# A block-local attention kernel: the last three slots of the last batch and all that follows get a written-out order on all five engines, over more PSUM banks

## The reference

```python
def attn(x, Wq, bq, Wk, bk, Wv, bv, Wo, bo):      # x: 8 x 1024 x 256, 16 heads of 16
    q, k, v = (x @ W.T + b, split into heads)
    scores = einsum('bqhd,bkhd->bhqk', q, k) * 0.25
    mask = (j <= i) & (j >= i - 128)
    scores = where(mask, scores, -10000.0)
    p = softmax(scores) + 1e-9
    return einsum('bhqk,bkhd->bqhd', p, v) @ Wo.T + bo
x = x + attn(layernorm(x), ...)
x = x + einsum('bsi,oi->bso', layernorm(x), sign(weight))
```

## Time and profile before

| | us |
|---|---|
| median of 3 runs | 717.18 |
| the runs | 714.24, 717.18, 721.31 |
| the profiled execution's time | 716.17 |
| its span in the trace | 714.4 |
| PE busy | 668.4 (94%) |
| DVE / ACT / POOL busy | 493.9 / 485.6 / 458.0 |
| mean granted TensorE clock | 0.992 |

### The profile page before, as it was taken

The page is one execution under the profiler, slowest core; times in us unless marked ns, Lnnn a source line. Parts: engine busy times, 40 slices in busy tenths (PEclk is TensorE's granted clock), DMA queues, the critical chain, the costliest instruction groups (busy, mean ns, idle before and its releaser), DMA issues.

```text
span 714.4 us, 31680 instructions
## 1 busy us (share of the span) xinstructions
PE 668.4 (94%) x13152; PEld 595.7 (83%) x13152; DVE 493.9 (69%) x1043; ACT 485.6 (68%) x1061; POOL 458.0 (64%) x651
## 2 busy tenths in 40 slices
PE   7789999999999999999999999999999999998875
PEld 6667988888888888898898888889898889886764
DVE  5566766777777767787777777777677877765435
ACT  4357776777768667777767677677667777674651
POOL 8936565677656567766666677566567756664662
PEclk9989999999999999999999999999999999999999
DMA  5948776796677677677676786767577757866411
GB/s 150 129 78 134 108 121 122 126 137 117 125 115 135 118 117 128 133 129 118 124 131 127 117 130 118 123 121 129 115 127 137 129 105 122 138 114 83 75 39 45
DMA packets 94942, 83.76 MB, mean 117 GB/s; under 512 B 10416, under 2 KB 94800, under 8 KB 94800
## 3 DMA queue, kind: packets, MB, share of 16 engines
q1 hardware_dynamic: 93354, 80.38, 65.8%
q10 hardware_dynamic: 1446, 1.35, 0.6%
HBM read 18.22 MB, written 8.39 MB: 37 GB/s over the span
## 4 chain that ended last, share of the span: by engine, by line
PE 73%; DMA 10%; SPq 6%; issue 4%; DVE 4%; ACT 2%; POOL 1%; DVEq 0%; POOLq 0%; ACTq 0%
PE gc L966 17%; PE sc L1102 16%; PE pv L1118 12%; PE ga L966 10%; DMA q_stack<-nmax_t 8%; SPq L271 5%; PE mx L1057 5%; PE mx L1063 4%; PE ga L1131 3%; PE gc L981 2%; DVE nmax L754 2%; PE gb L1146 2%; PE gb L1166 2%; DMA q_stack<-q_hi 1%; DVE x L814 1%
## 5 line engine op out<-in xcount | busy, mean ns | idle before, releaser
L561 ACT ACTIVATE prob<-sc 128x512 f32<-128x512 f32 x448 | 259.5, 599 | 103.3 <-PE sc L1102 99.5
L754 DVE TENSOR_REDUCE nmax<-mx 128x6 f32<-128x960 f32 x189 | 197.1, 1043 | 68.0 <-PE mx L1063 64.8
L1102 PE MATMUL sc<-q_stack,k_stack 128*128 128x256 f32 (+1 forms) x1024 | 210.8, 304 | 8.6 <-DMA q_stack<-nmax_t 3.5
L1102 PEld LDWEIGHTS sc<-q_stack,k_stack 128*128 128x128 f32 x1024 | 150.0, 191 | 24.5 <-DMA q_stack<-nmax_t 8.3
L434 POOL TENSOR_SCALAR ve<-mv 128x1 f32<-128x1 f32 x64 | 14.2, 222 | 206.5 <-DVE mv L826 205.3
L419 POOL TENSOR_SCALAR_AFFINE_SELECT prob<-prob 128x1024 f32<-128x1024 f32 x128 | 140.0, 1093 | 1.7 <-ACT prob L563 1.7
L416 POOL TENSOR_SCALAR_AFFINE_SELECT prob<-prob 128x1024 f32<-128x1024 f32 x112 | 122.4, 1093 | 11.9 <-ACT prob L561 11.6
L1118 PE MATMUL pv<-prob,v_ones 128*32 128x128 f32 x3840 | 119.6, 274 | 2.9 <-issue 2.2
L1118 PEld LDWEIGHTS pv<-prob,v_ones 128*32 128x32 f32 x3840 | 101.5, 110 | 12.2 <-issue 2.9
L1063 PE MATMUL mx<-k_max,q_stack 16*32 16x160 bf16 x4032 | 71.1, 229 | 3.3 <-issue 3.3
L792 DVE TENSOR_TENSOR ct_lo<-gb,ct_hi 128x256 fp32r<-128x256 f32 x64 | 26.8, 419 | 46.1 <-ACT ct_hi L578 46.1
(11 more groups left out here) (169 smaller groups left out, 1410.5 us busy)
## 6 DMA issues: line engine op xcount, KB each, us to landing
q_stack<-q_hi SPq DMA_DIRECT2D x128, 128.0 KB, 3.9
k_stack<-k_hi SPq DMA_DIRECT2D x128, 128.0 KB, 4.6
xs<-x SPq DMA_DIRECT2D x32, 256.0 KB, 4.2
q_stack<-q_lo SPq DMA_DIRECT2D x64, 128.0 KB, 4.9
k_stack<-k_lo SPq DMA_DIRECT2D x64, 128.0 KB, 4.4
xr<-x SPq DMA_DIRECT2D x64, 128.0 KB, 2.1
out<-x SPq DMA_DIRECT2D x64, 128.0 KB, 2.4
k_max<-k SPq DMA_DIRECT2D x64, 64.0 KB, 3.5
```

The lines of the kernel that those rows point to most:

```text
L561: a.activation(prob[:, own:nxt + 1:nxt - own, 2 * f:2 * f + 2, :], sc, ACT.Exp, scale=SCALE).then_inc(exp_done, 1)
L754: v.tensor_reduce(nmax[:, n % 2, :].rearrange("p (r h) -> p r h", r=C)[:, :, h0:h0 + m], banks[:, :, 0:WIN * m].rearrange("p r (h k) -> p ...
L1102: last = mm(sc_bank[f % 2][:, 2 * P * j:2 * P * j + q], k_stack[:, h, ak:ak + P], q_stack[:, h % HB, P * t:P * t + q], start=True, stop=True)
```

## The change

The slots of the last batch are run only up to slot 4 (`ENDING = 5`). For slots 5, 6, 7 and what follows, each of the five engines has one written-out list of calls. No instruction of the computation is added or taken away; what differs is their order, the banks and the waits that go with the banks:
- `turn_u` of tiles 2, 3 and 4 writes to `gc` (before: `ga`), as tiles 5 to 7 already did. Its wait is then for cx of the tile before, in place of x2 of the tile before.
- `turn_x2` of tiles 1, 2 and 3 writes to `late_t2` (before: `gb`), `second_layer` of these tiles to `late_ff` (before: `ga`). `out_proj` then waits only for x2 of the tile before, not for its finish.
- `prob_v` of tile 7 writes to `late_pv`, which is score bank 0, and waits there for the exponentials 0 to 6 of tile 7, in place of `sums` of tile 6.
- `turn_c` late also waits for the last row maxima's copy (`nm_done`), which comes early in slot 5.
- On POOL `mask_probs` is split into `mask_next` and `mask_own`, and the lists put the own mask before the next mask in most places.
- On SP `stack_k` of the last pair is ahead of `load_xr` of tile 3, and stores and loads follow each other as listed.

The diff, with context cut:

```diff
@@ -39,6 +39,7 @@
 AHEAD = 4
+ENDING = 5
@@ -138,6 +139,7 @@
         late_t2, late_ff = mx_banks[:, 0, :], mx_banks[:, 1, :]
+        late_pv = sc_bank[0]
@@ -227,7 +229,7 @@
             for b in range(BATCHES):
-                for t in range(TILES):
+                for t in range(TILES if b < LAST else ENDING):
                     slot(b, t)
@@ -302,6 +304,12 @@
                 sp.dma_start(xr[:, i], x_tile[b, t]).then_inc(xr_loaded[i], 16)
+
+            def store_y(b, t):
+                i, _ = halves(t)
+
+                sp.wait_ge(y_done, TILES * b + t + 1)
+                sp.dma_start(y_tile[b, t], x2[:, i]).then_inc(y_stored[i], 16)
@@ -319,10 +327,7 @@
                 if part["ff"]:
-                    bb, tt = part["ff"]
-                    i, _ = halves(tt)
-                    sp.wait_ge(y_done, TILES * bb + tt + 1)
-                    sp.dma_start(y_tile[bb, tt], x2[:, i]).then_inc(y_stored[i], 16)
+                    store_y(*part["ff"])
                 if (b, t) == (0, 0):
@@ -342,8 +347,20 @@
             run(sp, slot)
-            for t in range(4):
-                slot(BATCHES, t)
+            stack_k(LAST, 3)
+            load_xr(LAST, 3)
+            stack_nmax(sp, LAST, 7)
+            load_xr(LAST, 4)
+            store_y(LAST, 1)
+            load_xr(LAST, 5)
+            store_y(LAST, 2)
+            load_xr(LAST, 6)
+            store_y(LAST, 3)
+            load_xr(LAST, 7)
+            store_y(LAST, 4)
+            store_y(LAST, 5)
+            store_y(LAST, 6)
+            store_y(LAST, 7)
             for i in range(2):
@@ -407,17 +424,27 @@
-            def mask_probs(b, t, r):
+            def mask_next(b, t, r):
                 n = TILES * b + t
                 pool.wait_ge(exp_done, SC_FILLS * n + 4 * (r + 1))
-                if t < TILES - 1:
-                    nxt = prob[:, 2 + n % 3, HB * r:HB * (r + 1), :]
-                    g.affine_select(out=nxt, in_=nxt, compare_op=ALU.is_ge, fill=0.0, base=0,
-                                    pattern=[[0, HB], [-1, P]], channel_multiplier=1)
+                nxt = prob[:, 2 + n % 3, HB * r:HB * (r + 1), :]
+                g.affine_select(out=nxt, in_=nxt, compare_op=ALU.is_ge, fill=0.0, base=0,
+                                pattern=[[0, HB], [-1, P]], channel_multiplier=1)
+
+            def mask_own(b, t, r):
+
+                n = TILES * b + t
+                pool.wait_ge(exp_done, SC_FILLS * n + 4 * (r + 1))
                 own = prob[:, n % 2, HB * r:HB * (r + 1), :]
                 g.affine_select(out=own, in_=own, compare_op=ALU.is_ge, fill=0.0, base=0,
                                 pattern=[[0, HB], [1, P]], channel_multiplier=-1).then_inc(prob_masked, 1)
+
+            def mask_probs(b, t, r):
+
+                if t < TILES - 1:
+                    mask_next(b, t, r)
+                mask_own(b, t, r)
@@ -449,8 +476,6 @@
                     add_biases(*part["op"])
-                if (b, t) == (LAST, TILES - 1):
-                    mask_probs(b, t, 1)
                 if part["op"]:
@@ -467,7 +492,25 @@
             run(pool, slot)
+            mask_own(LAST, 4, 1)
+            add_biases(LAST, 2)
+            mask_own(LAST, 5, 0)
+            add_biases(LAST, 3)
+            mask_next(LAST, 4, 1)
+            mask_own(LAST, 5, 1)
+            mask_next(LAST, 5, 0)
+            mask_own(LAST, 6, 0)
+            mask_next(LAST, 5, 1)
+            rsqrt2(LAST, 2)
+            add_biases(LAST, 4)
+            mask_own(LAST, 6, 1)
+            mask_next(LAST, 6, 0)
+            rsqrt2(LAST, 3)
+            mask_next(LAST, 6, 1)
             add_biases(LAST, 5)
+            rsqrt2(LAST, 4)
+            mask_own(LAST, 7, 0)
+            mask_own(LAST, 7, 1)
             add_biases(LAST, 6)
@@ -584,12 +627,12 @@
-            def sums(b, t):
+            def sums(b, t, bank=pv_bank):
                 n = TILES * b + t
                 act.wait_ge(pv_filled, n + 1)
                 wait(act, ut_filled, n - 1)
-                a.activation(u[:, t % 2, :], pv_bank[:, :], ACT.Copy).then_inc(u_done, 1)
+                a.activation(u[:, t % 2, :], bank[:, :], ACT.Copy).then_inc(u_done, 1)
@@ -692,13 +735,47 @@
             run(act, slot)
+            nmax_part(LAST, 7)
+            exp(LAST, 5, 0)
+            exp(LAST, 5, 1)
+            exp(LAST, 5, 2)
+            exp(LAST, 5, 3)
+            exp(LAST, 5, 4)
+            first_hi(LAST, 2)
+            second_hi(LAST, 1, late_t2)
+            exp(LAST, 5, 5)
+            exp(LAST, 5, 6)
+            sums(LAST, 4)
+            exp(LAST, 5, 7)
+            exp(LAST, 6, 0)
+            exp(LAST, 6, 1)
+            exp(LAST, 6, 2)
+            first_hi(LAST, 3)
+            second_hi(LAST, 2, late_t2)
+            exp(LAST, 6, 3)
+            sums(LAST, 5)
+            exp(LAST, 6, 4)
+            exp(LAST, 6, 5)
+            exp(LAST, 6, 6)
+            first_hi(LAST, 4)
+            exp(LAST, 6, 7)
+            second_hi(LAST, 3, late_t2)
+            exp(LAST, 7, 0)
+            exp(LAST, 7, 1)
+            exp(LAST, 7, 2)
+            sums(LAST, 6)
+            exp(LAST, 7, 3)
+            first_hi(LAST, 5)
+            exp(LAST, 7, 4)
+            exp(LAST, 7, 5)
             second_hi(LAST, 4, late_t2)
-            first_hi(LAST, 5)
-            sums(LAST, 7)
+            exp(LAST, 7, 6)
+            exp(LAST, 7, 7)
             first_hi(LAST, 6)
             second_hi(LAST, 5, late_t2)
+            sums(LAST, 7, late_pv)
+            second_hi(LAST, 6, late_t2)
             first_hi(LAST, 7)
-            second_hi(LAST, 6, late_t2)
             second_hi(LAST, 7, late_t2)
@@ -934,24 +1011,42 @@
             run(dve, slot)
+            normalise(LAST, 2, gc)
+            second_lo(LAST, 1, late_t2)
+            first_lo(LAST, 2)
+            normalise(LAST, 3, gc)
+            residual(LAST, 2)
+            stats2(LAST, 2)
+            finish(LAST, 1, late_ff)
+            normalise(LAST, 4, gc)
+            second_lo(LAST, 2, late_t2)
+            first_lo(LAST, 3)
+            residual(LAST, 3)
+            first_lo(LAST, 4)
+            stats2(LAST, 3)
+            finish(LAST, 2, late_ff)
             normalise(LAST, 5, gc)
-            second_lo(LAST, 4, late_t2)
+            second_lo(LAST, 3, late_t2)
+            residual(LAST, 4)
+            finish(LAST, 3, late_ff)
+            stats2(LAST, 4)
             first_lo(LAST, 5)
             normalise(LAST, 6, gc)
+            second_lo(LAST, 4, late_t2)
+            residual(LAST, 5)
+            first_lo(LAST, 6)
+            stats2(LAST, 5)
             finish(LAST, 4, late_ff)
-            residual(LAST, 5)
-            stats2(LAST, 5)
-            first_lo(LAST, 6)
             second_lo(LAST, 5, late_t2)
+            residual(LAST, 6)
             normalise(LAST, 7, gc)
-            residual(LAST, 6)
+            finish(LAST, 5, late_ff)
+            second_lo(LAST, 6, late_t2)
+            first_lo(LAST, 7)
             stats2(LAST, 6)
-            finish(LAST, 5, late_ff)
-            first_lo(LAST, 7)
-            second_lo(LAST, 6, late_t2)
             residual(LAST, 7)
+            finish(LAST, 6, late_ff)
             stats2(LAST, 7)
-            finish(LAST, 6, late_ff)
             second_lo(LAST, 7, late_t2)
@@ -1103,19 +1198,22 @@
-            def prob_v(b, t):
+            def prob_v(b, t, bank=pv_bank):
                 n = TILES * b + t
                 if n == 0:
                     pe.wait_ge(memset_done, 2)
                 pe.wait_ge(prob_masked, 2 * n + 2)
-                wait(pe, u_done, n)
+                if bank is pv_bank:
+                    wait(pe, u_done, n)
+                else:
+                    pe.wait_ge(exp_done, SC_FILLS * n + 7)
                 terms = [(t - 1, 2 + (n - 1) % 3), (t, n % 2)][0 if t > 0 else 1:]
                 for cg in range(4):
                     for k, (tile, part) in enumerate(terms):
                         for j in range(4):
                             h = 4 * cg + j
-                            last = mm(pv_bank[32 * j:32 * (j + 1), P * cg:P * (cg + 1)], v_ones[:, tile, h, :], prob[:, part, h, :],
+                            last = mm(bank[32 * j:32 * (j + 1), P * cg:P * (cg + 1)], v_ones[:, tile, h, :], prob[:, part, h, :],
                                       start=cg == 0 and k == 0, stop=cg == 3 and k == len(terms) - 1, skip_group_check=True)
@@ -1137,6 +1235,7 @@
                     pe.wait_ge(ct_lo_done, n)
+                    pe.wait_ge(nm_done, NT)
                 else:
@@ -1379,20 +1478,63 @@
             run(pe, slot)
+            turn_max(LAST, 7)
+            scores(LAST, 5, 0)
+            turn_u(LAST, 2, gc)
+            scores(LAST, 5, 1)
+            turn_x2(LAST, 1, None, late_t2)
+            scores(LAST, 5, 2)
+            scores(LAST, 5, 3)
+            turn_c(LAST, 2, True)
+            scores(LAST, 5, 4)
+            turn_u(LAST, 3, gc)
+            scores(LAST, 5, 5)
+            scores(LAST, 5, 6)
```

(43 more changed lines are left out.)

## The result

| | before | after |
|---|---|---|
| median of 20 runs, us | 719.43 | 712.01 |
| lowest, highest | 714.24, 725.28 | 705.60, 715.15 |
| profiled execution: time, span | 716.17, 714.4 | 706.15, 704.3 |
| mean granted clock of that execution | 0.992 | 0.991 |

The changed kernel is faster by less than 1%: ratio 0.9928, 95% interval 0.9904 to 0.9953, which is some 5.2 us. The medians of the same 20 and 20 executions differ by 7.4 us, their means by 8.1. The measured median lies inside the range, 3.6 us above the forecast of 708.4. The gain by the ratio is 0.7%. Forecast were 8.8 us or 1.2% of 717.2; against the median before in this comparison, 719.43, the forecast time would be 1.5% less.

The account below looks back on a forecast made before the run. From slot 5 of the last batch the bound was taken to be the order of hand-overs between engines. Gains of 2.6 us up to exp(7,7) and 6.2 behind it, 8.8 together, took 717.2 to 708.4 us; range 704 to 714.

Parts of the forecast that it names:

- term B: From the end of exp(7,7) to the end: dependent path of tile 7 takes 13.0 us against 19.83; gain 6.2 us.
- slow stores: Rival: four stores in the ending's chain take 3.6 us each, holding residuals of tiles 4 to 7; 712.2 us, chance 0.10.
- Nothing ahead of M: Up to 669.6 us, before slots 5 to 7, instructions, sizes and counts are the same; change costed at nothing.
- Term A: Slots 5 to 7: exp(7,7) ends earlier as PE waits less; 3.5 us by the lists, 2.6 taken.
- the walk: New lists of five engines followed from 669.6 us, each call at the latest of queue and waits; PE waits 1.0 us.
- The order catches: Rival: hand-overs on PE up to scores(7,7) cost more than priced; gain 0 + 5 us, 712.2 us, chance 0.15.
- given back ahead of the mark: Rival: work is moved but not saved, -3.2 us before exp(7,7) ends and 6.1 behind; 714.3 us, chance 0.11.
- The move on SP: stack_k ahead of load_xr: column maxima for tile 7 near 671 instead of 674.38, well before scores(6,0); no cost.
- The masks on POOL: Masks end just before prob_v needs them: 678.4 for tile 5 at 678.8, 685.1 for tile 6 at 685.3.
- the chain of four: Four stores between finish of tile 2 and residual of tile 7; at 1.7 us each all are met.
- the 0.95: Sign of being wrong: a granted clock under 0.95 in the ending.
- The rival's large form: Rival: a gap in slot 6 drops the clock to 1.2 GHz for some 20 us of PE work; 728 us, chance 0.04.

Follow-up runs that it names:

- banks_only: The kernel before in its own order, with the new banks and their waits in slots 5 to 7 of the last batch: 719.76 us, ratio 0.9978.
- sp_old: The changed kernel, but on SP load_xr of tile 3 comes ahead of stack_k of the last pair again: 715.7 us, ratio 0.9947.
- before_again: The kernel before, unchanged, run again for a second trace; its repeats against itself gave ratios of 0.9962 and 1.000.
- banks_only_2: A repeat of the kernel before in its own order with the new banks in slots 5 to 7: 718.96 us, ratio 1.0001.

## Why the prediction was right or wrong

The kinds of wait that the prediction named are the ones that went. What failed is a size: term B, the part behind exp(7,7), 6.2 us in the forecast and 4.5 in the traces, because the slow stores were charged as a case of their own and not in the term, and because the base had one in it. The time missed as well by its base, 717.18, which was 3.0 us low.

- **Nothing ahead of M.** Right: 556 to 559 us in every trace from the 7th mark to the 61st. But the profiled execution after is 10.1 us shorter than the one before, and 1.7 of these lie ahead of M, by chance.
- **Term A, 2.6 us.** Measured 3.0 (from 25.0 to 22.0; the third trace of before has 26.5, since `prob_v` of tile 6 ran at half clock there). Counted from M, scores(7,7) start at 21.2 us where the walk had 20.6, prob_v(6) at 16.4 for 15.7. The deduction of 0.9 for thin margins was a little too much. "The order catches" and "given back ahead of the mark" did not happen. (The first of these rivals counts 5 us behind exp(7,7) where term B has 6.2, and gives no reason.) That new banks keep PE dense was not enough as a reason: banks_only has the banks and no gain.
- **The move on SP, costed at nothing with the words "well before it is due".** The cost was right, since PE does not wait for the maxima in any of the three traces of the changed kernel, but the reason was not, and that it came right was in part luck. The new order brings scores(6,0) forward by 2.3 us from M (7.2 in place of 9.5). The maxima are issued 2.2 us behind M. With the 3.9 to 5.0 us from issue to use of the other traces they arrive, by my estimate, 0 to 1.1 us before they are due. The cover was made by the moved line itself. I had no row for the landing and took it to be short. Its price without cover, "one for one", was too low as well: in sp_old 2.5 us of waiting became 4.2 with a stretch of half clock behind it.
- **The masks on POOL.** Right: in the trace after, the own mask ended 0.5 us before prob_v(5) and 0.3 before prob_v(6), and their old order costs 1.4 us.
- **Term B, 6.2 us: the step that failed.** Too large; measured 4.5 on average (19.1 to 14.6). The path of 13.0 us was right: 13.1 to 13.2 in the four traces of its kind in which no residual waited for a store. Two parts were mis-sized. First the base: 19.83 us was one execution in which a store of 3.59 us had held DVE for 1.2; the other two traces of before have 18.7. Against 18.7 the path of 13.0 could gain 5.7 at most. (Even there a store of usual length is in the chain: in before_again `residual` of tile 7 waits 1.17 us for one of 1.73.) Second the stores, where the prediction says "At 1.7 us all are met": I saw the chain of four, gave "slow stores" 0.10 as a case in which all four are slow, and left the case of one slow store as the lower bound of the term, 4.3. In all three traces of the changed kernel exactly one of the four was slow, the one with 0.2 us of slack in the walk, and it cost 0.8, 1.5 and 1.5 us, so that the term came out near its lower bound. The prediction's estimate of 2.3 us for a store, from the Trainium skill, DMA: Bandwidth & Descriptors, section on the anatomy of one DMA, leans to the right side but fits neither kind of store here: the usual one took 1.7 us, the slow one 2.8 to 3.5. That section's figures are for DMAs that GpSimd issues, and these stores are issued on SP.
- **The new bank for `prob_v` of tile 7**, which I let count in B: worth nothing.
- **The sum**: 8.8 forecast, 8.0 by the traces (3.0 + 4.5, and 0.5 for the half clock in one trace of before), 8.5 plus or minus 1.2 by all executions, 5.2 by the ratio of the first comparison. The means of that comparison's own executions give 8.1, the later ratios of the same two kernels 0.9875 and 0.9899, and no run shows a mechanism that would give anything back; why that ratio is lower stays open.
- **The time, 708.4.** Its base was the median of three runs, 717.18, and the median of 105 executions is 720.2. That is 3.0 of the 3.6 us by which 712.01 exceeds the forecast.
- **The clock.** It fell for the last 3 to 5 us of all three traces of the changed kernel. In the first (0.83 over the last 14.8 us, under the 0.95 that I had named as a sign of being wrong) the fall came ahead of the last two pairs of matmuls and cost 0.5 us, in the second it touched the last pair (0.1 us), in the third it cost nothing. So my sentence that gaps of a microsecond do not do it does not hold: PE's longest wait in that stretch of the first trace is 0.93 us. All three traces of before have waits as long (0.95) there and kept the full clock to their last matmul. What decides between the two is not shown. The rival's large form, 20 us of PE work at half clock, came in no trace. Stretches of 3 to 7 us ahead of exp(7,7) came in sp_old, banks_only, banks_only_2 and also in before_3.

## What to carry to other kernels

Walking the written lists of all engines from one mark gave the dependent path to 0.1 us and the dense part to 0.6; what it missed were the landing of a DMA for which it had no row, and how often one store in a chain is slow. So look up the landing of every DMA that a step brings nearer to its use, and ask whether a change on another queue is what makes it arrive. In a chain with several stores, charge one slow store where the slack is smallest, not all or none: here it was that one in three traces of three, and in four of the nine that have the new order on PE. A base from one profiled execution carries its own mishaps, and where a kernel spreads by 10 us, differences of 1 us can be read only between marks inside the traces.

## What the runs showed of the hardware

- A store of 128 KB took 1.7 us from issue to landing in most cases of the last 40 us, 2.0 to 2.5 in some and 2.8 to 3.6 in others. The slow ones of the ending came with the DMA engines almost idle (share 0.14 in after).
- The stacked maxima, 8 KB behind the six loads of the stacked keys, took 3.9 to 5.0 us from issue to use in the six traces in which PE or its weight load waited for them (the three of before, banks_only, banks_only_2, sp_old).
- PE stops behind the 52nd of the 64 matmuls of `prob_v` in slot 3 of the last batch for 1.6 to 2.2 us in every trace of every kernel, and ACT and DVE wait for it; the profile names no releaser, and the cause stays open. In nine of the 14 traces the granted clock was at half for 3 to 7 us behind it.
- The granted clock between 30 and 60 us differed from 0.67 to 0.89 between executions of the same code, and the start with it, by up to 9 us.
